# An expert layer whose inner values are formed transposed, a token mix moved off the tensor engine, and first tokens spread over more steps

## The reference

```python
# layer 0, token mix (RWKV)
x_prev = jnp.pad(x[:, :-1, :], ((0, 0), (1, 0), (0, 0)))
xk = x * time_mix_k + x_prev * (1.0 - time_mix_k)      # xv and xr alike
k = jnp.einsum('bth,oh->bto', xk, W_k)                 # v alike
r = jax.nn.sigmoid(jnp.einsum('bth,oh->bto', xr, W_r))
wkv = _wkv_full(k, v, time_decay, time_first)          # a scan over the 256 tokens
out = jnp.einsum('bth,oh->bto', r * wkv, W_o)

# layer 0, experts
xn = _rms_norm(x, scale)
ids = jnp.argmin(_dist2(xn, centroids), axis=-1)       # one of 8 experts for each token
for e in range(N_EXPERTS):
    h = jnp.einsum('bsd,dh->bsh', xn, up_w[e])         # 128 -> 512
    a, g = jnp.split(h, 2, axis=-1)
    y = jnp.einsum('bsh,hd->bsd', a * jax.nn.silu(g), down_w[e])   # 256 -> 128
    out = jnp.where((ids == e)[..., None], y, out)
return out + skip
```

## Time and profile before

| what | value |
|---|---|
| time, median of 3 runs | 1221.29 us (1216.65 to 1221.37) |
| time of the profiled execution | 1218.42 us |
| its span | 1216.7 us |
| PE busy / DVE / ACT / POOL | 1068.0 us (88%) / 959.5 us (79%) / 880.9 us (72%) / 791.2 us (65%) |
| layer zero ends, layer one begins | at 392.2 us of the span |

### The profile page before, as it was taken

How to read it: one execution, slowest core, us unless ns; L and a number is a source line. 1 busy time by engine, 2 the same in 40 slices (tenths; PEclk the granted TensorE clock), 3 DMA queues, 4 the chain that set the end, 5 groups by cost and what they waited for, 6 DMA issues and landing times.

```text
span 1216.7 us, 29072 instructions
## 1 busy us (share of the span) xinstructions
PE 1068.0 (88%) x8602; PEld 682.5 (56%) x8603; DVE 959.5 (79%) x2148; ACT 880.9 (72%) x2187; POOL 791.2 (65%) x1147
## 2 busy tenths in 40 slices
PE   2766369999987589999999999999999999999985
PEld 1655246667764355555655565555655565555642
DVE  6678988888996477888788878888888887888861
ACT  2555338777765368888888888888888888888874
POOL 4476767666786266667766776677667766776630
PEclk9866679999998699999999999999999999999998
DMA  9611111111211332233323322332233223322310
GB/s 247 175 41 37 33 54 49 47 45 46 58 42 34 81 89 65 66 91 83 78 65 92 86 74 68 92 86 72 70 90 90 68 73 86 88 71 74 81 37 11
DMA packets 148166, 89.27 MB, mean 73 GB/s; under 512 B 73080, under 2 KB 137272, under 8 KB 147768
## 3 DMA queue, kind: packets, MB, share of 16 engines
q1 hardware_dynamic: 143928, 79.01, 25.4%
q0 software_dynamic: 4096, 8.53, 2.5%
HBM read 55.91 MB, written 31.47 MB: 72 GB/s over the span
## 4 chain that ended last, share of the span: by engine, by line
PE 51%; issue 6%; DVE 4%; ACT 4%; SPq 1%; DMA 1%; POOL 0%; DVEq 0%; POOLq 0%
PE PS L1943 8%; PE PS L1933 6%; PE PS L1919 5%; PE PS L2008 5%; PE PS L2030 5%; ACT PT L1793 3%; DVE bm L1583 3%; PE PS L2022 3%; PE PS L1995 3%; PE PS L1985 3%; PE PS L1957 3%; PE PS L1889 3%; PE PS L1973 3%; PE PS L2039 2%; PE PS L1897 1%
## 5 line engine op out<-in xcount | busy, mean ns | idle before, releaser
L1583 DVE TENSOR_REDUCE bm<-PS 128x16 f32<-128x1024 f32 x256 | 312.4, 1220 | 32.9 <-PE PS L1919 25.2
L1793 ACT ACTIVATE PT<-PS 128x1024 f32<-128x1024 f32 x256 | 262.5, 1025 | 22.2 <-PE PS L1933 18.6
L1943 PE MATMUL PS<-PT,rows 128*32 128x256 f32 x2048 | 137.9, 387 | 1.7 <-ACT OT L1798 1.7
L1472 POOL TENSOR_TENSOR Pr<-Pr,linv 128x512 f32<-128x512 f32 x128 | 131.9, 1042 | 5.0
L1767 ACT ACTIVATE Pr<-PS,nmf 128x256 f32<-128x256 f32 x256 | 117.5, 475 | 0.0
L1933 PE MATMUL PS<-QS,KS 51*128 51x256 bf16 x1024 | 100.0, 273 | 13.6 <-ACT PT L1793 8.4
L1603 DVE TENSOR_REDUCE nmf<-PS 128x4 f32<-128x1024 f32 x64 | 78.4, 1225 | 42.4 <-PE PS L2008 42.4
L1919 PE MATMUL PS<-KS,QS 48*128 48x256 bf16 x1024 | 101.3, 276 | 10.1 <-DVE bm L1583 6.0
L476 POOL DMA_INDIRECT xs_dram<-rows,slot x64 | 66.1, 1032 | 40.3 <-DVEq L704 22.6
L1011 PE MATMUL PS<-S,wmix 128*128 128x256 f32 (+1 forms) x192 | 70.2, 452 | 16.8 <-DVE diff L732 16.3
L1985 PE MATMUL PS<-xT,wsel 128*128 128x256 f32 x256 | 74.6, 416 | 8.6 <-DMA wsel<-in_qkv_w 7.8
(11 more groups left out here) (258 smaller groups left out, 2830.6 us busy)
## 6 DMA issues: line engine op xcount, KB each, us to landing
wsel<-in_qkv_w SPq DMA_DIRECT2D x128, 96.0 KB
parts_dram<-parts SPq DMA_DIRECT2D x32, 384.0 KB
QS<-parts_dram SPq DMA_DIRECT2D x64, 96.0 KB
KS<-parts_dram SPq DMA_DIRECT2D x64, 96.0 KB
xs_dram<-zero_t SPq DMA_DIRECT2D x1, 4752.0 KB, 27.2
xs_t<-xs_dram SPq DMA_DIRECT2D x72, 66.0 KB, 1.8
ys_dram<-ys_t SPq DMA_DIRECT2D x72, 64.0 KB, 1.6
QS<-parts_dram SPq DMA_DIRECT2D x64, 64.0 KB
```

The lines of the kernel that those rows point to most:

```text
L1472: pool.tensor_tensor(Pr[i][:, qt, :, :], Pr[i][:, qt, :, :], linv[:, i, qt, :].unsqueeze(2).broadcast_to([P, 2, SEQ]), ALU.mult).then_inc( ...
L1583: dve.tensor_reduce(bm[:, i // 2, :, 2 * (i % 2):2 * (i % 2) + 2, :].rearrange("p q r b -> p r q b"), bS.rearrange("p (r q b k) -> p r q b ...
L1793: act.activation(PT[i % 4][:, :, :], bT.rearrange("p (r k) -> p r k", r=2), ACT.Exp).then_inc(s_exp, 1)
L1943: last = pe.matmul(bC[j * VC:(j + 1) * VC, 0:SEQ], V2[q][:, kt, 4 * g + j, :], PT[(2 * g + j // 2) % 4][:, j % 2, kt * SEQ:(kt + 1) * SEQ] ...
```

## The change

The diff does five things.

1. **Experts.** The rms factor is applied by ACT to a tile's rows before the transpose (`xsr`, k = 0, from SBUF to SBUF); transpose and copy `xsT` come at k = 1, and the copy now carries the rms scale per feature. The up product comes at k = 2, as four 128x128 products with a piece of the weights as the stationary operand, so the inner values lie in PSUM with hidden features on partitions and tokens along the row. tanh is at k = 2, the gate at k = 3, and the down product at k = 4 takes `hid` as it is: the two transposes, the copy `hidT`, and the one-time scaling of all up weights are gone. The up weights no longer lie in SBUF; SP loads the 128x512 weights of a tile's expert (256 KB) by a DMA with a register offset into one of four buffers, one turn before the tile begins.
2. **Receptance.** The mix of a token and its predecessor is formed before the product: ACT writes `mixed` and `share` (two 128x256 activations at lag 3), POOL adds them (`mix`, after `weigh`, at lag 3), and PE multiplies once at lag 4 instead of twice.
3. **First tokens.** Their work starts at step 20 in place of 28 and is spread over steps 20 to 31, one or two instructions a step.
4. **Loop.** The hardware loop is written out.
5. **Layer one.** The `KS` rows are filled in steps 1 to 4, after `load_qk`, and in the last batch `shifted_scores` and `exp_scores` alternate between two pairs of banks.

The scatter now waits for the zeroed rows and the down weights together, since their semaphores are shared.

```diff
@@ layer zero
-        STATIC = 16
-        TAIL = 28
-        TAKE = 28
+        TAKE = 20
-        up = sb("up", [P, NE * 2 * HID])
+        up = [sb(f"up{i}", [P, 2 * HID]) for i in range(NUP)]
+        mixed = two("r_mixed", [P, SEQ])
+        share = two("r_share_of_previous", [P, SEQ])
-            for s in range(first, STATIC):
-                step(s // NQ, s % NQ)
-            with eng.Fori(STATIC // NQ, TAIL // NQ) as quad:
-                for p in range(NQ):
-                    step(quad, p)
-            for s in range(TAIL, END + 3):
+            for s in range(first, END + 3):
                 step(s // NQ, s % NQ)
@@ sync
-            sp.dma_start(up[:, :], up_w).then_inc(s_we, 16)
-            sp.dma_start(down[:, :], down_w).then_inc(s_we, 16)
+            sp.dma_start(down[:, :], down_w).then_inc(s_zero, 16)
             def load(t, h, q):
-                after(sp, s_fx, t - 2)
+                after(sp, s_xsr, t - 2)
+            def load_up(t, h, q):
+                after(sp, s_up, t - NUP + 1)
+                sp.load(expert_registers[q % TPS], tile_expert[0:1, bass.ds(t, 1)])
+                e = sp.snap(expert_registers[q % TPS], min_val=0, max_val=NE - 1)
+                apart(sp)
+                sp.dma_start(up[q % NUP][:, :], up_w[:, bass.ds(e * 2 * HID, 2 * HID)]).then_inc(s_upl[q % NUP], 16)
@@ gpsimd
+            def mix(t, q):
+                pool.wait_ge(s_rs, t + 1)
+                pool.tensor_tensor(mixed[q % 2][:, 1:SEQ], mixed[q % 2][:, 1:SEQ], share[q % 2][:, 1:SEQ], ALU.add).then_inc(s_rx, 1)
+            def first_tokens(s):
+                for t in range(NFIRST):
+                    at = s - TAKE - 3 * t
+                    if at in (0, 1):
+                        first_rows(t, at)
+                    if at == 5:
+                        first_residual(t)
+                    if at in (7, 8):
+                        first_norm(t, at - 7)
                 skip(quad, p, 1)
+                first_tokens(s)
                 if runs(m[0]) and not early(m[0]):
                     products(pool, *m)
                 if runs(d[0]):
@@
                 if runs(w[0]):
                     weigh(*w)
+                    mix(*w)
@@ vector
-                now = tile(quad, p, turn, 2)
+                now = tile(quad, p, turn, 3)
@@ scalar
+            def shares(t, q):
+                act.wait_ge(s_xnT, t + 1)
+                after(act, s_rp, t - 1)
+                after(act, s_rx, t - 1)
+                act.activation(mixed[q % 2][:, :], xnT(t), ACT.Identity, scale=cols[:, 4:5])
+                act.activation(share[q % 2][:, 1:SEQ], xnT(t)[:, 0:SEQ - 1], ACT.Identity, scale=ommix[:, 2:3]).then_inc(s_rs, 1)
                 if runs(b[0]):
                     keys_values(*b)
+                if runs(e[0]):
+                    shares(*e)
                 experts(quad, p, 2)
@@ tensor
             def receptance(t, q):
                 pe.wait_ge(s_kv, most(t + 3))
-                project(t, 2, psR, s_rp)
+                pe.wait_ge(s_rx, t + 1)
+                pe.matmul(psR, w0[:, 2, :], mixed[q % 2][:, :], start=True, stop=True).then_inc(s_rp, 1)
-                now = tile(quad, p, turn, 3)
-                    for c in range(2):
-                        last = pe.transpose(psH[:, c * P:(c + 1) * P], hid[q % 3][:, c * P:(c + 1) * P], ident[:, :])
-                now = tile(quad, p, turn, 1)
+                now = tile(quad, p, turn, 2)
-                    pe.matmul(psU[q % 2][:, :], xsT[q % 3][:, :], up[:, bass.ds(e * 2 * HID, 2 * HID)],
-                              start=True, stop=True).then_inc(s_up, 1)
+                    for c in range(2 * HID // P):
+                        last = pe.matmul(psU[q % 2][:, c * P:(c + 1) * P], up[q % NUP][:, c * P:(c + 1) * P], xsT[q % 3][:, :],
+                                         start=True, stop=True)
+                    last.then_inc(s_up, 1)
@@ layer one, sync and tensor
+                    if batch1[0] < NQ:
+                        load_minus_rows(batch1[0])
-                after(pe, s_exp, HP * t + i)
+                if t == B - 1:
+                    pe.wait_ge(s_exp, HP * t + i - (i > 0))
+                    pe.wait_ge(s_red, HP * B)
+                else:
+                    after(pe, s_exp, HP * t + i)
```

More of the change, by code:

```diff
@@ L181, in layer_zero @@
         TPS = 3
+        NUP = 4
         G = NQ * TPS
@@ L250, in layer_zero @@
         xsT = three("xsT", [P, P])
-        gate, hid, hidT = ([work[:, (3 * k + i) * HID:(3 * k + i + 1) * HID] for i in range(3)] for k in range(3))
+        gate, hid, xsr = ([work[:, (3 * k + i) * HID:(3 * k + i + 1) * HID] for i in range(3)] for k in range(3))
         ys_t = three("ys_t", [P, D])
@@ L436, in step @@
                         load(*new)
+                    soon = tile(quad, p, turn, -1)
+                    if soon and (not isinstance(soon[0], int) or soon[0] >= 1):
+                        load_up(*soon)
                     done = tile(quad, p, turn, LAST)
@@ L627, in setup @@
                 dve.wait_ge(s_setv, 1)
-                for j in range(3):
+                for j in range(2):
                     dve.tensor_scalar(wmix[:, 0, j, :], w0[:, j, :], cols[:, 2 + j:3 + j], None, ALU.mult)
@@ L893, in experts @@
             def experts(quad, p, turn):
-                now = tile(quad, p, turn, 0)
+                now = tile(quad, p, turn, 1)
                 if now:
@@ L898, in experts @@
                     after(act, s_up, t - 2)
-                    act.copy(xsT[q % 3][:, :], psX[:, 0:P]).then_inc(s_xsT, 1)
-                now = tile(quad, p, turn, 3)
-                if now:
-                    t, h, q = now
-                    act.wait_ge(s_fh, t + 1)
-                    after(act, s_dn, t - 2)
-                    act.copy(hidT[q % 3], psH[:, 0:2 * P]).then_inc(s_hidT, 1)
+                    act.activation(xsT[q % 3][:, :], psX[q % 2][:, 0:P], ACT.Identity, scale=scale_c[:, 0:1]).then_inc(s_xsT, 1)
                 now = tile(quad, p, turn, 4)
@@ L910, in experts @@
                     after(act, s_ys[q % 3], arrivals(h, q) - 16)
-                    act.activation(ys_t[q % 3][:, :], psY[:, 0:D], ACT.Identity, scale=xs_t[q][:, D + 1:D + 2]).then_inc(s_y, 1)
-                now = tile(quad, p, turn, 1)
+                    act.activation(ys_t[q % 3][:, :], psY[:, 0:D], ACT.Identity, scale=0.5).then_inc(s_y, 1)
+                now = tile(quad, p, turn, 0)
+                if now:
+                    t, h, q = now
+                    act.wait_ge(s_xs[q % 3], arrivals(h, q))
+                    after(act, s_fx, t - 2)
+                    act.activation(xsr[q % 3][:, 0:D], xs_t[q][:, 0:D], ACT.Identity, scale=xs_t[q][:, D:D + 1]).then_inc(s_xsr, 1)
+                now = tile(quad, p, turn, 2)
                 if now:
@@ L1193, in layer_one @@
         o_t = two("o_t", [P, TB, D])
-        s_neg = sem("minus_one_rows_loaded")
+        s_neg = [sem(f"minus_one_rows_loaded{i}") for i in range(NQ)]
         s_slot = first.s_slot
@@ L1308, in _, with load_minus_rows @@
         def _(sp):
-            for i in range(NQ):
+            def load_minus_rows(i):
                 for j in range(2):
```

134 lines of the change are left out of this document (62 added, 72 removed).

## The result

| | kernel before | changed kernel |
|---|---|---|
| time, median | 1221.33 us (1216.65 to 1222.94) | 1347.83 us (1346.42 to 1351.26) |
| span of the profiled execution | 1216.7 us | 1349.5 us |
| `bb` of step 12, of step 35 | 181.61, 383.95 us | 185.81, 519.74 us |
| a step, mean of these 23 | 8.80 us | 14.52 us |

The ratio is 1.104, with a 95% interval of 1.101 to 1.107: slower by 126 us. I had forecast 1254 us and 1280 as the upper end. The spans differ by 132.8 us: step 12 comes 4.2 us later, the 23 steps to step 35 take 131.6 us more, the rest of the program 3.0 less. So the loss lies where I had looked for it, and is three times as large.

The account below looks back on a forecast made before the run. PE was the fullest engine; the new wait for `mix` would close a chain of 10.4 us a step against 8.80. 1218.42 + 37 + 2 - 3.5 - 3 + 3 = 1254 us, range 1222 to 1280.

Parts of the forecast that it names:

- The experts' part: Layer zero's tiles: split up product costs the same, PE 1.1 us a step shorter, up weights by DMA cost 0.
- The chain through `mix`: PE's receptance waits for POOL's mix, closing a loop once a step: 10.4 us against 8.80, 37 us more.
- the prediction's own last sign: The forecast fails if PE is found not to wait for POOL's mix.
- The clock's share: PE's half clock after gaps ahead of the receptance: 1.2 us in each of three steps, 3 us.
- Rival A: PE's clock falls in most steps: same chain plus 1.2 us in 20 steps, 1275 us; chance 12%.
- Intake: Scatter and first expert rows later through copy, shares and mix: 2 us more, bounds 0 and 4.
- ACT's shares: Two new 128x256 activations, 0.42 us each, hidden by ACT's room of 2.2 us a step.
- First tokens: Their work, some 4 us before, lies in POOL's waiting, 3.3 us a step; uncovered it costs 4 us again.
- Layer one: Head weights issued sooner, -3.5 us (bounds -1 and -4); last batch's exponentials, -3 us (bounds 0 and -4).
- Loop: Writing out the hardware loop: 0 us, bounds -2 and 2.
- The up product in four pieces: On PE, eight passes of 128 columns take 0.88 us, as two of 512 did: no difference.

Follow-up runs that it names:

- e1: Changed kernel with SP issuing the finished tile's store ahead of the loads of rows and up weights in each turn; 1263.07 us, ratio 1.043.
- e4: Changed kernel with the store first on SP and the receptance as two products again, without shares and mix; 1195.43 us, ratio 0.986.
- e11: Changed kernel with SP's order in a turn as load of rows, store, load of up weights; 1274.63 us, ratio 1.044.
- e9: Kernel before with its loop written out and, of the change, only the receptance (shares, mix, one product); 1281.42 us, ratio 1.051.
- e10: Kernel before with its loop written out, nothing else; 1216.68 us, ratio 0.997.
- e8: e4 with the first tokens' work begun at step 22 in place of 20; 1188.64 us, ratio 0.982.
- e5: e1 with ACT's shares one step sooner (lag 2) and POOL's mix ahead of its products; 1219.60 us, ratio 1.007.

## Why the prediction was wrong

The direction was right by another cause than the one forecast: in this kernel the ring through the stores sets the pace, and the wait for `mix` that was to make it slower is hidden. In per cent of the kernel before, opening the ring gives back 6.15 (e1) and the receptance then 5.64 (e4); what is left of the change is 1.38 faster than before. The 10.4 measured are 6.15 + 5.64 - 1.38.

**The experts' part: wrong, by a step that I left out.** "They are issued when the tile before has been scaled and are needed three turns later, a whole step. I take 0." I asked whether the up weights come in time (they do: none of the changed kernel's long waits is for them) and never what the new DMA and the new wait stand in front of. On SP the order in a turn is load, up weights, store. Two edits worked together: `load` now waits for `xsr` in place of PE's transpose, and `xsr` was written behind `ys_t` on ACT. This closed the ring, 4.63 us a turn; the up weights put ahead of the store made 1.6 of it (e11), enough to take it from 9.0 us a step, under the other limits, to 13.9. e1 against the changed kernel prices it: 6 of the 10.4%, some 75 us. The timeline before had what was needed: a store 1.6 us from issue to landing, three `ys_t` buffers, and SP's order in the code.

**The chain through `mix`: right in mechanism and nearly in length, hidden by the longer ring.** In the changed kernel PE waits for `mix` in three steps of 23, and by the prediction's own last sign that is its failure; e1 and e9 show the chain with the forecast's terms. Alone it costs more than was forecast: from e10 to e9 a step grows by 2.50 us and not by 1.6. Of the 0.9 us between, 0.26 are a longer chain (10.66 for 10.4), 0.20 are e10's shorter step (8.60 for 8.80), and 0.44 are steps beyond 10.66, most of them at half clock. The clock's share was mis-sized: three steps at 1.2 us were taken, 3 us in all. In e1 the granted clock is 0.91 from step 12 to 35. Without the one step in which the first tokens wait (17.5 us) the mean is (256.6 - 17.5)/22 = 10.87 us, and the chain with an up product at full clock is 10.48 (the terms above, 1.62 in place of 2.50): 0.39 x 23 = 9 us. In e9 (11.10 - 10.66) x 23 = 10, of which the 8 steps at half clock are 7.

**Clock.** In the changed kernel it is 0.83 over the stretch, in which PE is idle for 116 of 334 us. It followed from the waits: e8, with the same up and down products and two more passes of the receptance, has 1.00. The Trainium skill ("TensorE: Matmul & The Clock Gate", HAM oscillation) says that bursts of matmuls between waits bring the half clock back again and again. The traces agree in a part of the steps: in e1 the granted clock of a step lies between 0.85 and 1.00 (0.69 in the one with the first tokens), and in the changed kernel between 0.67 and 0.97. Rival A, to which I had given 12%, had it in most steps.

**Intake: too small.** Forecast + 2, bounds 0 to 4. Step 12 came 4.2 us later. e9 against e10 gives 4.9 for the receptance alone, e1 against e4 6.0; the ring adds 2.2 (the changed kernel against e1), and the rest of the change brings step 12 forward by 3.9 (e4). Each is one trace against another, and the kernel before with its loop written out (e10) has step 12 0.9 us sooner on another chip.

**ACT's shares: not hidden.** e5 leaves 0.9 us a step.

**First tokens: wrong.** I placed them in POOL's waiting time and did not ask what they wait for. At step 20 they make the step 10 us longer in the changed kernel and 5 us in e4; from step 22 on no step of e8 is longer for them.

**Layer one: right in the sum** (4.6 and 2.7 us; forecast 3.5, with 4 as its bound, and 3). **Loop:** 3 us gained, forecast 0, bound 2. **The up product in four pieces: right.** At full clock the changed kernel's eight passes of 128 columns are one piece of 1.06 us, as eight times 0.11 and a tail (in two other places of its trace, at 185.32 and 197.38, the next product starts 0.89 us after such a piece; the forecast had 0.88):

```profile
257.36 1.06 PE L1091 MATMUL PS<-xsT,up 128*128 128x128 f32 x8
```

## What to carry to other kernels

When an edit makes a queue wait for something else, write down everything that stands behind that wait on the queue, and who waits for it: a queue that issues both loads and stores ties the input of new tiles to the output of old ones, and with few output buffers this closes a ring. Put the stores, which wait for finished work, ahead of the loads: what counts is the wait that they no longer stand behind, since in e1 they land no sooner (2.6 us). Price a pipeline by its longest ring and not by a sum of parts, since taking out a shorter one shows next to nothing: the receptance gave 0.5% before the ring was open and 5.6% after.

## What the runs showed of the hardware

- A store of 64 KB issued 0.45 us behind a load of 256 KB on the same queue landed after 2.5 to 2.7 us (median; changed kernel 2.5, e1 2.6, e8 2.7). Issued 0.4 us behind a load of 66 KB and ahead of the 256 KB it landed after 1.7 (e11), and where no such weights are loaded, after 1.6 (kernel before).
- From the issue of the rows' load to that of the up weights, with a register load (0.27 us) between, SP takes 0.89 us; without one, from one issue to the next, 0.4 to 0.45 (changed kernel, e11).
- An interrupted rhythm costs twice. In e1 PE waits for `mix` in nearly every step, 1.1 to 1.4 us in most, and in 11 of 23 steps the up product behind that wait is at half clock in whole or in part; at its longest (2.05 us for 1.13) it makes the chain longer by 0.9 us. In e8, without that wait, the granted clock is 1.00.
